# Cross-attention and mixture-of-experts block on one core: first head group's rows by tripled products, batch 1 projected later, value biases added once

## The chip, the cores and the metric

The kernel runs on one core of a Trainium2 chip. The metric is device microseconds of one execution; the value given for a kernel is the median of several runs.

## What is computed

Input x is 4 batches of 256 tokens with 128 channels, ctx is 4 batches of 64 tokens with 64 channels. All in float32; cut to what matters:

```
xn = layernorm(x)                                 # (4, 256, 128)
q, k, v = heads(xn@Wq+bq), heads(xn@Wk+bk), heads(xn@Wv+bv)        # 16 heads of 8
y  = softmax(causal(q k^T / sqrt(8))) v
qc, kc, vc = heads(xn@Wcq+bcq), heads(ctx@Wck+bck), heads(ctx@Wcv+bcv)
y += softmax(qc kc^T / sqrt(8)) vc
x1 = x + y@Wp + bp
x2 = layernorm(x1)
out = x1 + shared_expert(x2) + sum over the top 8 of 32 experts(x2)   # sigmoid router
```

## The kernel before, in words

Every product that must keep float32 precision is made of three matmuls on a rounded part ("hi") and a remainder ("lo"): hi*hi, hi*lo, lo*hi (`product3`, L1417 to L1419). So each operand is first rounded by ScalarE (`round_x`, `round_qkc`) and its remainder made by VectorE (`split_x`, `split_qkc`, which read the same PSUM bank).

**Steps.** Attention runs in 16 steps i = 4 b + g (batch b, group g of 4 heads). For one step the keys of 4 heads stand in `key_rows` (96 rows: hi, hi, lo of 32 channels) and the queries in `query_rows` (96 rows: hi, lo, hi, and 4 more rows for the shift by the row maximum). The products of a projection come out as channels x tokens in `keys` and `queries`; DMAs (`place_keys`, `place_queries`, three each for a batch and group) copy them into the rows. Context keys go by `place_ctx_keys` into `ckey_rows`. `expand(i)` multiplies the key rows by a mask per head, two heads on ScalarE and two on VectorE (POOL from step 5), and gives `key_blocks`; `expand_ctx(g)` does it for the context keys.

On TensorE, `natural(i)` makes the scores with the tokens of the queries on the partitions: tile 0 in bank B_NAT0, tile 1 in two banks, the context in B_NATC. VectorE's `maxima(i)` reduces the three (`row_max`, L1145, L1149, L1154). `turn_max(i)` (L1560) turns the maxima, ScalarE's `shift(i)` (L836) writes them into `query_rows`, `scores(i, c)` (L1574, L1579, L1583) makes the transposed scores in four parts c, and ScalarE's `exps` (L844) the probabilities. POOL's two selects clear what is above the diagonal. `attend_self`, `attend_context` (L1599 to L1611) multiply by the values, one step late. So TensorE's order in the loop is: scores(i, 0 and 1), turn_max(i+1), natural(i+2), scores(i, 2 and 3), a tail, attend(i-1). `tail_at` holds the tails: in step 0 `x_pair` (the last two batches' normalized x turned, and rounded by ScalarE), in steps 1 to 4 the projections of batches 2 and 3 (`keys_queries`, `cross_values`). The experts' part follows after step 15.

**Before step 0.** Batch 0 is projected, its rows placed by DMA (keys of group 0 by SP, queries of group 0 by ScalarE and SP, the other keys of batch 0 and all context keys from POOL's queue, the other queries from SP's). Then `natural(0)`, then all of batch 1's projections (`project(1)`), then `turn_max(0)`. The matmuls on `fill` (`run_idle`, L1457) compute nothing that is used. The norms of x are VectorE's for batches 0 and 1 (L1040) and ScalarE's for the rest (L884, after the fourth and in the midst of step 0). VectorE adds the value biases, broadcast over partitions by DMA, to every value product (L1077).

Every engine takes its instructions in the order written; waits are on semaphores.

Of the kernel before, what the change touches and what calls it, by code (L numbers as in the profile page):

```python
# [5 lines left out]
F32 = mybir.dt.float32  # L6
# [39 lines left out]
BIAS_Q, BIAS_K, BIAS_CQ, BIAS_CK = range(2 * UNITS, 2 * UNITS + 4)  # L46
BIAS_ROWS = 2 * UNITS + 4
# [23 lines left out]
B_QKC, B_VALUE, B_BIAS, B_CK = 4, 7, 2, 3  # L71
B_CV = B_OUT


FIRST_BATCHES = 2


def build(nc, x, ctx, w, out):

    with ExitStack() as stack:  # L80
# [19 lines left out]
        head_mask = sb("head_mask", [P, GROUP])  # L100
# [6 lines left out]
        w_qkv_lo = sb("w_qkv_lo", [P, 5, C], F32R)  # L107
        w_ctx = sb("w_ctx", [CTX_C, 2, C])
# [82 lines left out]
        in_wide = sem("in_wide")  # L191
# [11 lines left out]
        rows_set = sem("rows_set")  # L203
        bias_rows_set = sem("bias_rows_set")
# [3 lines left out]
        ckey_rows_set = sem("ckey_rows_set")  # L208
        zeroed = sem("zeroed")
# [27 lines left out]
        v_ckey_blocks_set = sem("v_ckey_blocks_set")  # L237
# [24 lines left out]
        have_ctxT2 = sem("have_ctxT2")  # L262
# [122 lines left out]
        def product_bank(b, n):  # L385

            if b < FIRST_BATCHES:
                return bank(B_QKC + n, SEQ)
            half = n % 2
            return psum[:, B_MISC, SEQ * half:SEQ * (half + 1)]  # L390

        def value_bank(b):

            half = b >= FIRST_BATCHES
            return psum[:, B_VALUE, SEQ * half:SEQ * (half + 1)]
# [26 lines left out]

        HALF = CHUNK // 2
# [3 lines left out]
        def rows_of_part(part):  # L427

            return slice(part, SHIFT_ROW, PARTS)

        def keys_of(b, g):

            if b == 0 and g:
                return pool_placed_k[g], 48
            return placed_k[b % 2][g], 48 * (b // 2 + (b % 2 == 1 or g == 0))

        def place_keys(eng, b, g, parts=range(PARTS)):

            mine = slice(PART * g, PART * (g + 1))
            for part in parts:  # L440
                half = KEY_PARTS[part]
                eng.dma_start(key_rows[rows_of_part(part), b % 2, g, :].bitcast(F32),
                              keys[mine, half, tokens(b)].bitcast(F32)).then_inc(keys_of(b, g)[0], 16)

        def place_queries(eng, b, g, parts=range(PARTS)):

            mine = slice(PART * g, PART * (g + 1))
            for part in parts:
                half = QUERY_PARTS[part]
                eng.dma_start(query_rows[rows_of_part(part), b % 2, g, :, :].bitcast(F32),  # L450
                              queries[mine, half, b, :, :].bitcast(F32)).then_inc(placed_q[b % 2][g], 16)

        def place_ctx_keys(eng, g):

            for part, half in enumerate(KEY_PARTS):
                eng.dma_start(ckey_rows[rows_of_part(part), g, :].bitcast(F32),  # L456
                              ckeys[PART * g:PART * (g + 1), half, :].bitcast(F32)).then_inc(placed_ck[g], 16)

        def key_block(i, j):
# [3 lines left out]
                    head_mask[0:ROWS, j:j + 1])  # L463
# [7 lines left out]
        def ckey_block(g, j):  # L471
# [3 lines left out]
                    head_mask[0:ROWS, j:j + 1])  # L475
# [34 lines left out]
        def _(sp):  # L510
# [15 lines left out]
            for n, name in enumerate(("bv", "bcv")):  # L526
                sp.dma_start(b_wide[:, n, :], row(w[name]).to_broadcast([P, C])).then_inc(in_wide, 16)
# [5 lines left out]
            sp.dma_start(bias_rows[BIAS_UP + PAIRS:BIAS_UP + UNITS, INNER:P], row(w["bu_s"])).then_inc(in_small, 16)  # L533

            sp.wait_ge(rows_set, 1)
            sp.wait_ge(qkc_rounded, 1)
            place_keys(sp, 0, 0, (0, 1))
            sp.wait_ge(qkc_split, 1)
            place_keys(sp, 0, 0, (2,))
            sp.wait_ge(qkc_split, 3)  # L540
            place_queries(sp, 0, 0, (1,))
            for g in range(1, GROUPS):
                place_queries(sp, 0, g)
# [8 lines left out]
            sp.dma_start(b_wide[:, 2, :], row(w["bp"]).to_broadcast([P, C])).then_inc(in_bp, 16)  # L552
# [14 lines left out]
        def _(pool):  # L567
# [29 lines left out]
            pool.wait_ge(x_normed, NORM_GROUPS[0][1])  # L597
            pool.memset(value[:, :, :, D:D + 1], 1.0).then_inc(zeroed, 1)
            pool.memset(ckey_rows[:, :, :].bitcast(F32), -1.0).then_inc(ckey_rows_set, 1)
            chain(pool.memset(cvalue[:, :, :, :], 0.0))  # L600
            first_rstd(1)
            pool.wait_ge(ck_rounded, 1)
            pool.wait_ge(ck_split, 1)
            pool.wait_ge(ckey_rows_set, 1)
            place_ctx_keys(pool, 0)
            pool.wait_ge(qkc_rounded, 1)
            pool.wait_ge(qkc_split, 1)
            place_keys(pool, 0, 1)
            first_rstd(2)
            place_ctx_keys(pool, 1)  # L610
            place_keys(pool, 0, 2)
            pool.wait_ge(have_rstd, 3)
            pool.memset(cvalue[0:CTX, :, :, D:D + 1], 1.0).then_inc(zeroed, 1)
            pool.wait_ge(zeroed, 2)
            pool.memset(cvalue[CTX:P, :, :, 32 + D:32 + D + 1], 1.0).then_inc(zeroed, 1)
            place_ctx_keys(pool, 2)
# [1213 lines left out]
```

## Time and profile before

| | us |
|---|---|
| median of 3 runs | 201.01 (200.78 to 201.4) |
| profiled execution, its own time | 201.61 |
| its span, from first to last instruction | 199.9 |

| engine | busy us | share of the span |
|---|---|---|
| PE (TensorE) | 187.5 | 94% |
| DVE (VectorE) | 148.6 | 74% |
| ACT (ScalarE) | 137.7 | 69% |
| POOL (GpSimd) | 111.4 | 56% |

The busy times are of the whole span. The granted TensorE clock over the span is 0.995 of full speed. 1.71 us of the profiled execution's time lie outside its span.

### The profile page before, as it was taken

What the parts mean: (1) busy time and instruction counts of PE and PEld (TensorE: products, weight loads), DVE (VectorE), ACT (ScalarE), POOL (GpSimd) and SP (SyncE); (2) the same over time, 40 slices, a digit from 0 to 9 for tenths busy, and PEclk for the clock granted to TensorE, in tenths of its full rate; (3) what the DMA queues carried; (4) which work ended last, traced back from release to release, by engine and by line L of the source; (5) the groups of instructions that cost most, each with busy time, mean ns of one, the idle gap of its engine ahead of it and who ended that gap; (6) DMA issues with size and microseconds to landing.
All of it is one profiled execution on the core that took longest, in us unless ns stands there. A gap on an engine that the chain in (4) does not pass through costs nothing.

```text
span 199.9 us, 4006 instructions
## 1 busy us (share of the span) xinstructions
PE 187.5 (94%) x1254; PEld 138.7 (69%) x1254; DVE 148.6 (74%) x343; ACT 137.7 (69%) x280; POOL 111.4 (56%) x181
## 2 busy tenths in 40 slices
PE   7969979999999999998999799699999999999993
PEld 2637657777777777765776678488788888887661
DVE  2999997677669765895692789549677888887982
ACT  3546879788898897987789375666655556555571
POOL 6889994556396699749737367685522333000020
PEclk9999999999999999999999999999999999999998
DMA  4354423222243223501111102030000000000003
GB/s 111 105 144 124 113 72 78 67 74 69 66 117 94 64 72 81 127 2 39 44 44 39 39 13 66 3 92 8 2 0 0 3 0 0 0 2 0 3 0 105
DMA packets 20434, 10.40 MB, mean 52 GB/s; under 512 B 11881, under 2 KB 18542, under 8 KB 20414
## 3 DMA queue, kind: packets, MB, share of 16 engines
q1 hardware_dynamic: 19290, 9.24, 18.4%
q0 software_dynamic: 672, 0.69, 1.4%
q10 hardware_dynamic: 452, 0.23, 0.5%
q8 instruction: 10, 0.16, 0.4%
q14 instruction: 10, 0.08, 0.1%
HBM read 4.51 MB, written 0.52 MB: 25 GB/s over the span
## 4 chain that ended last, share of the span: by engine, by line
PE 71%; DVE 12%; POOL 6%; issue 4%; ACT 4%; DMA 2%; DVEq 0%
PE psum L1417 10%; PE psum L1418 10%; PE psum L1419 10%; PE psum L1518 5%; PE psum L1574 5%; PE psum L1611 4%; PE psum L1599 4%; PE psum L1621 3%; DVE gated L1361 3%; PE psum L1517 3%; PE psum L1579 3%; PE psum L1747 3%; PE psum L1457 2%; POOL ckey_rows L456 2%; PE psum L1583 2%
## 5 line engine op out<-in xcount | busy, mean ns | idle before, releaser
L982 ACT ACTIVATE gate<-psum,bias_cols 128x512 f32<-128x512 f32 (+2 forms) x35 | 23.5, 675 | 29.1 <-PE psum L1419 29.0
L844 ACT ACTIVATE probs<-psum 128x512 f32<-128x512 f32 x64 | 36.3, 596 | 2.3 <-PE psum L1579 1.2
L1361 DVE SCALAR_TENSOR_TENSOR gated<-psum,bias_cols,gate 128x512 f32<-128x512 f32 x32 | 24.0, 749 | 13.7 <-ACT gate L982 12.9
L738 POOL TENSOR_TENSOR hid_lo<-hid,hid_hi 128x512 fp32r<-128x512 f32 x13 | 16.8, 1289 | 30.4 <-ACT hid_hi L991 30.4
L1518 PE MATMUL psum<-key_blocks,query_rows 96*128 96x512 f32 x48 | 24.1, 544 | 0.0
L1373 DVE TENSOR_TENSOR hid<-gated,psum 128x512 f32<-128x512 f32 x32 | 21.9, 683 | 2.0 <-PE psum L1747 0.2
L657 POOL TENSOR_TENSOR w_late_lo<-w_ffn,w_late_hi 128x384 fp32r<-128x384 f32 x11 | 12.7, 1158 | 17.4 <-ACT w_late_hi L856 17.4
L991 ACT CAST hid_hi<-hid 128x512 fp32r<-128x512 f32 (+1 forms) x33 | 20.2, 612 | 1.2 <-DVE hid L1379 0.6
L1145 DVE TENSOR_REDUCE row_max<-psum 128x4 fp32r<-128x512 f32 x16 | 11.0, 688 | 13.4 <-PE psum L1518 13.4
L1149 DVE TENSOR_REDUCE row_max<-psum 128x4 fp32r<-128x1024 f32 x16 | 19.4, 1214 | 0.0
L1417 PE MATMUL psum<-xT_hi,w_late_hi 128*128 128x512 f32 x42 | 16.7, 398 | 0.0
L1418 PE MATMUL psum<-xT_lo,w_late_hi 128*128 128x512 f32 x42 | 16.4, 391 | 0.0
L693 POOL TENSOR_SCALAR_AFFINE_SELECT probs<-probs 128x512 f32<-128x512 f32 x16 | 10.2, 635 | 11.2 <-ACT probs L844 11.0
L1419 PE MATMUL psum<-xT_hi,w_late_lo 128*128 128x512 f32 x42 | 16.4, 390 | 0.0
L851 ACT COPY o_sb<-psum 128x512 f32<-128x512 f32 x16 | 9.4, 585 | 9.3 <-PE psum L1611 9.2
L781 ACT ACTIVATE key_blocks<-key_rows,head_mask 100x256 fp32r<-100x256 f32 x32 | 14.4, 499 | 1.8 <-DMA key_rows<-keys 1.8
L1031 DVE TENSOR_TENSOR hid_lo<-hid,hid_hi 128x512 fp32r<-128x512 f32 (+2 forms) x22 | 14.4, 658 | 1.0 <-ACT hid_hi L991 0.9
L697 POOL TENSOR_SCALAR_AFFINE_SELECT probs<-probs 128x512 f32<-128x512 f32 x16 | 10.2, 634 | 8.5 <-ACT probs L844 8.3
L1517 PE MATMUL psum<-causal,ident_bf 128*128 128x512 bf16 x32 | 12.5, 389 | 1.8 <-DVE key_blocks L1051 1.5
L684 POOL TENSOR_TENSOR key_blocks<-key_rows,head_mask 100x256 fp32r<-100x256 f32 x22 | 13.1, 615 | 0.0
L1747 PE MATMUL psum<-routeT,spread 128*128 128x512 f32 x32 | 12.8, 401 | 0.0
L1457 PE MATMUL psum<-fill 128*128 128x512 bf16 x33 | 11.0, 458 | 1.3 <-DVE fill L1064 1.3
(208 smaller groups left out, 513.5 us busy)
## 6 DMA issues: line engine op xcount, KB each, us to landing
query_rows<-queries SPq DMA_DIRECT2D x46, 64.0 KB, 2.1
key_rows<-keys SPq DMA_DIRECT2D x39, 32.0 KB, 1.9
w_ffn<-in_L_ffn_Wg SPq DMA_DIRECT2D x16, 64.0 KB, 2.0
w_ffn<-in_L_ffn_Wu SPq DMA_DIRECT2D x16, 64.0 KB, 2.2
w_ffn<-in_L_ffn_Wd SPq DMA_DIRECT2D x16, 64.0 KB, 2.1
ckey_rows<-ckeys POOLq DMA_DIRECT2D x12, 32.0 KB, 2.1
key_rows<-keys POOLq DMA_DIRECT2D x9, 32.0 KB, 2.2
x_sb<-in_x SPq DMA_DIRECT2D x2, 128.0 KB, 2.8
```

Source lines behind the costliest of these rows:

```text
L844: act.activation(probs[:, i % 2, c, :], bank(B_ST + c % 2), ACT.Exp, scale=SCALE).then_inc(exp_done, 1)
L982: act.activation(gate[rows_of(n), n % 3, part], psum[of, B_GATE + n % 2, part], ACT.Silu, bias=bias_cols[of, BIAS_GATE + u:BIAS_GATE + u + ...
L991: act.copy(hid_hi[rows_of(n - 1), (n - 1) % 3, :], hid[rows_of(n - 1), (n - 1) % 3, :]).then_inc(hid_rounded, 1)
L1149: dve.tensor_reduce(to[:, 1, :], psum[:, B_NAT1:B_NAT1 + 2, :].rearrange("p k (j c) -> p j k c", j=GROUP), AX.XY, ALU.max).then_inc(max_do ...
L1361: dve.scalar_tensor_tensor(out=gated[:, n % 3, :], in0=bank(B_UP + n % 2), scalar=bias_cols[:, BIAS_UP + u:BIAS_UP + u + 1], in1=gate[:, n ...
L1373: dve.tensor_tensor(hid[:, n % 3, :], gated[:, n % 3, :], bank(B_WIDE + n % 2), ALU.mult).then_inc(hid_done, 1)
L1417: pe.matmul(dst, w_hi, x_hi, start=start, stop=False, skip_group_check=True)
L1418: pe.matmul(dst, w_hi, x_lo, start=False, stop=False, skip_group_check=True)
L1419: return pe.matmul(dst, w_lo, x_hi, start=False, stop=stop, skip_group_check=True)
L1517: pe.matmul(to, ident_bf[:, :], causal[:, :, :], start=True, stop=False, skip_group_check=True)
L1518: return pe.matmul(to, query_rows[0:KR, b % 2, g, 0, P * q:P * (q + 1)], blocks[:, :, P * k:P * (k + 1)], start=not diagonal, stop=True, s ...
L1747: pe.matmul(bank(B_WIDE + n % 2), spread[:, u, :], routeT[:, c * CHUNK:(c + 1) * CHUNK], start=True, stop=True).then_inc(m_wide, 1)
```

## The change

1. **Rows of step 0 without DMA.** `w_direct_hi/lo` hold the first 32 columns of Wk, Wq and Wcq three times. `project_direct(k)` multiplies them by batch 0's x, so that 96 rows come out as `key_rows` and `query_rows` of group 0 want them; `round_direct` (ScalarE) writes all 96 rows, `split_direct` (VectorE) overwrites the 32 rows that hold the remainder. Two sets of bias columns are turned, one repeated. Group 0's row order becomes part by part, so `head_mask` has two forms (`masks()`, now at VectorE's start).
2. **Queues.** SP places context keys 0 and 3, keys 1 to 3, queries 2 and 3 of batch 0; POOL places context keys 1 and 2 and queries 1. ScalarE places none.
3. **Order at the start.** Context-key product ahead of the first projection; weight remainders of Wcq and Wv on POOL; batch 1's x normalized by ScalarE, turned inside `natural(0)`; the values of batch 0 copied by ScalarE; the shift of step 0 turned and written in two halves (`first_turn`, `first_shift`).
4. **Batch 1 projected later.** `project_qkc(1, n)` stands between scores(0, 1) and natural(1); its values and the context values are a tail of step 0; `x_pair` becomes the tail of step 1; each projection of batches 2 and 3 moves one step later (steps 2 to 5). ScalarE's four norms for batches 2 and 3 move into step 1, the statistics of those batches on VectorE behind split_qkc(1, 2), their power on POOL behind the selects of step 0.
5. **Value biases.** Values are copied without a bias; `y_bias` = bv + bcv as a column is added where y is rounded and split (`y_turn`). The two broadcast loads become two rows of `bias_rows`.

The core of the diff:

```diff
-        tail_at = {0: [("x_pair", FIRST_BATCHES)]}
-        for b in range(FIRST_BATCHES, BATCH):
-            tail_at[2 * b - 3] = [("keys_queries", b)]
-            tail_at[2 * b - 2] = [("cross_values", b)]
+        tail_at = {0: [("values", 1)], 1: [("x_pair", 2)]}
+        for b in range(2, BATCH):
+            tail_at[2 * b - 2] = [("keys_queries", b)]
+            tail_at[2 * b - 1] = [("cross_values", b)]
...
@@ ScalarE, start
+            round_direct(0)
+            round_direct(1)
+            round_qkc(0, 0)
+            expand(0)
+            round_qkc(0, 1)
+            round_qkc(0, 2)
+            round_direct(2)
...
+            def first_shift(s):
+                act.wait_ge(t_max, s + 1)
+                act.copy(query_rows[SHIFT_ROW:ROWS, 0, 0, s, :],
+                         psum[0:GROUP, B_MAX, SEQ * s:SEQ * (s + 1)]).then_inc(shift_placed, 1)
...
-            shift(0)
+            act.wait_ge(have_neg_mean, 1)
+            norm(2)
+            norm(3)
+            expand_ctx(0)
+            round_x(1)
+            act.wait_ge(m_v, 1)
+            act.wait_ge(zeroed, 1)
+            act.copy(value[:, 0:2, :, 0:D],
+                     value_bank(0).rearrange("p (t h d) -> p t h d", t=2, h=HEADS)).then_inc(have_value, 1)
+            first_shift(0)
+            expand(1)
             expand_ctx(1)
-            exps(0, (0, 1))
+            exps(0, (0,))
+            first_shift(1)
+            exps(0, (1,))
             expand(2)
-            act.wait_ge(have_neg_mean, 1)
-            norm(4)
-            norm(5)
+            for n in range(3):
+                round_qkc(1, n)
             exps(0, (2, 3))
             shift(1)
-            norm(6)
-            norm(7)
             for i in range(STEPS - 2):
                 if i:
                     exps(i, (0,))
                     shift(i + 1)
                     exps(i, (1,))
+                if i == 1:
+                    act.wait_ge(have_neg_mean, 2)
+                    for t in range(4, TILES):
+                        norm(t)
                 if i + 3 < STEPS:
                     expand(i + 3)
...
@@ VectorE
+            split_direct(0)
+            split_direct(1)
+            dve.wait_ge(rows_set, 1)
+            dve.wait_ge(have_mask, 1)
+            expand(0)
+            negative_mean(1)
+            split_qkc(0, 0)
...
@@ VectorE, maxima(0)
                 tile_0()
                 if i == 0:
+                    split_qkc(0, 1)
+                    split_qkc(0, 2)
                     dve.wait_ge(m_nat, 2)
                     tile_1()
-                    values(1)
+                    split_x(1)
+                    dve.wait_ge(t_ffn_bias, 1)
+                    dve.tensor_copy(bias_cols[:, 0:LATE_BIAS_ROWS],
+                                    psum[:, B_MISC, SEQ:SEQ + LATE_BIAS_ROWS]).then_inc(have_ffn_bias, 1)
+                    split_direct(2)
+                    expand(1)
                     dve.wait_ge(m_nat, 3)
                     context()
...
             maxima(0)
+            maxima(1)
+            expand(2)
             for n in range(3):
                 split_qkc(1, n)
...
+            stats_of(2)
             for i in range(STEPS):
                 if i + 3 < POOL_BLOCKS:
                     expand(i + 3)
+                if i == 0:
+                    negative_mean(2)
                 if i + 2 < STEPS:
                     maxima(i + 2, i - 2)
...
@@ POOL, loop over the steps, after the selects
+                if i == 0:
+                    first_rstd(2)
+                    expand_ctx(3, range(GROUP))
+                    pool.wait_ge(pool_ckey_blocks_set, 12)
...
@@ TensorE, natural(0) between its tiles and its context part
+                    pe.wait_ge(qkc_split, 1)
+                    run_idle(3, B_ST)
+                    pe.wait_ge(in_small, 96)
+                    pe.transpose(psum[:, B_MISC, SEQ:SEQ + LATE_BIAS_ROWS], bias_rows[:, :],
+                                 ident[0:LATE_BIAS_ROWS, 0:LATE_BIAS_ROWS]).then_inc(t_ffn_bias, 1)
+                    turn_x(1)
+                    pe.wait_ge(qkc_split, 3)
+                    project_values(0)
+                    run_idle(3, B_ST)
+                    first_turn(0)
+                    pe.wait_ge(direct_split, 3)
...
@@ TensorE, main
             natural(0)
-            project(1)
-            turn_max(0)
-            run_idle(3, B_MISC)
+            run_idle(2, B_ST)
             for i in range(STEPS):
-                if i == 0:
-                    pe.wait_ge(qkc_split, 3 * FIRST_BATCHES)
                 scores(i, 0)
                 scores(i, 1)
                 if i == 0:
+                    pe.wait_ge(xT_split, 2)
+                    pe.wait_ge(have_ffn_bias, 1)
+                    project_qkc(1, 0)
+                    project_qkc(1, 1)
+                    pe.wait_ge(have_value, 1)
+                    project_qkc(1, 2)
                     natural(1)
-                    context_values()
-                    scores(0, 2)
                     scores(0, 3)
```

In `natural(1)` the second half of step 0's maxima is turned behind tile 0, and scores(0, 2) stands ahead of tile 1. `tail("values", 1)` is `project_values(1)` and `context_values()`.

## Rows read from the trace of the kernel before

**Rows 1.** The page: shares of the chain of waits by engine.
```profile
PE 71%; DVE 12%; POOL 6%; issue 4%; ACT 4%; DMA 2%; DVEq 0%
```

**Rows 2.** Stretches: length, busy of PE, PEld, DVE, ACT, POOL; clock; DMA share, GB/s.
```profile
7.40:14.80 7.40, 5.89 (x34) 3.61 (x34) 7.13 (x34) 3.74 (x9) 6.23 (x10) 1.00 0.46 109
14.80:19.50 4.70, 4.64 (x31) 3.26 (x31) 4.16 (x10) 2.79 (x8) 4.64 (x12) 1.00 0.52 133
19.50:28.60 9.10, 7.98 (x48) 5.45 (x48) 8.65 (x18) 7.77 (x17) 8.92 (x17) 1.00 0.38 97
28.60:140.00 111.40, 107.29 (x885) 80.64 (x886) 79.35 (x200) 87.95 (x184) 74.22 (x121) 1.00 0.24 59
```

**Rows 3.** The chain that ended last, in order of time: start, us, what.
```profile
20.95 3.65 DMA key_rows<-keys
...
26.13 0.69 DVE row_max L1145
...
28.60 0.40 PE psum L1560 x4
...
31.09 0.12 PE psum L1417
...
33.12 0.67 PE psum L1574 x4
```

**Rows 4.** Timeline of TensorE: start, us, engine, line, operation, tiles, count, idle before.
```profile
8.29 0.70 PE L1479 MATMUL psum<-ctxT,w_ctx 64*128 64x256 f32 x2
...
14.79 0.38 PE L1517 MATMUL psum<-causal,ident_bf 128*128 128x512 bf16 x1 [1.51 <-DVE key_blocks L1051]
...
19.54 0.74 PE L1574 MATMUL psum<-query_rows,key_blocks 100*128 100x256 f32 x4
...
26.38 0.60 PE L1633 MATMUL psum<-ident,x 128*128 128x128 f32 x4
```

**Rows 5.** Timeline of VectorE, 11 to 26 us.
```profile
11.36 0.86 DVE L1022 BATCH_NORM_STATS2 stats<-x_sb 128x6 f32<-128x128 f32 x4
...
12.67 0.17 DVE L1027 TENSOR_SCALAR var_eps<-moments 128x4 f32<-128x4 f32 x1
...
18.61 0.86 DVE L1086 SCALAR_TENSOR_TENSOR queries<-psum,bias_cols,queries 128x256 fp32r<-128x256 f32 x2
19.39 0.15 DVE L1288 SCALAR_TENSOR_TENSOR neg_mean<-moments,rstd 128x4 f32<-128x4 f32 x1
19.46 0.61 DVE L1051 TENSOR_SCALAR key_blocks<-key_rows,head_mask 100x256 fp32r<-100x256 f32 x2
...
24.62 1.48 DVE L1051 TENSOR_SCALAR key_blocks<-key_rows,head_mask 100x256 fp32r<-100x256 f32 x2 [0.39 <-DMA key_rows<-keys]
```

**Rows 6.** Timeline of ScalarE, 25 to 32 us.
```profile
25.27 0.88 ACT L884 ACTIVATE x<-x_sb,neg_mean,rstd 128x128 f32<-128x128 f32 x2
26.05 0.89 ACT L781 ACTIVATE key_blocks<-key_rows,head_mask 100x256 fp32r<-100x256 f32 x2
...
29.04 0.57 ACT L836 CAST query_rows<-psum 4x512 fp32r<-4x512 f32 x1 [0.94 <-PE psum L1560]
29.64 0.60 ACT L844 ACTIVATE probs<-psum 128x512 f32<-128x512 f32 x1
30.14 0.90 ACT L781 ACTIVATE key_blocks<-key_rows,head_mask 100x256 fp32r<-100x256 f32 x2
30.93 1.07 ACT L844 ACTIVATE probs<-psum 128x512 f32<-128x512 f32 x2
31.89 0.48 ACT L808 ACTIVATE keys<-psum,bias_cols 128x256 fp32r<-128x256 f32 x1
```

**Rows 7.** Timeline of POOL, 13 to 28 us.
```profile
13.82 1.21 POOL L590 TENSOR_TENSOR rstd<-var_eps,minus_half 128x4 f32<-128x4 f32 x1
...
22.97 4.74 POOL L625 TENSOR_TENSOR ckey_blocks<-ckey_rows,head_mask 100x256 fp32r<-100x256 f32 x8
```

**Rows 8.** Timeline of SP's queue, issue of three DMAs of key rows.
```profile
18.77 1.77 SPq L442 DMA_DIRECT2D key_rows<-keys  x3
```

More of the change, by code:

```diff
@@ L449, in place_queries, with place_ctx_keys @@
                 half = QUERY_PARTS[part]
[L450 to L456, printed above, removed]
+                eng.dma_start(query_rows[rows_of_part(part, g), b % 2, g, :, :].bitcast(F32),
+                              queries[mine, half, b, :, :].bitcast(F32)).then_inc(queries_of(b, g)[0], 16)
+        def place_ctx_keys(eng, g, parts=range(PARTS)):
+            for part in parts:
+                half = KEY_PARTS[part]
+                eng.dma_start(ckey_rows[rows_of_part(part, g), g, :].bitcast(F32),
                               ckeys[PART * g:PART * (g + 1), half, :].bitcast(F32)).then_inc(placed_ck[g], 16)
@@ L1018, in chain, with measure @@
                 dve.wait_ge(v_chain, chained[0])
-            def norm_stats(src, tiles, done):
+            def measure(src, tiles):
                 for k in range(tiles.start, tiles.stop):
@@ L1023, in norm_stats, with spread_of @@
                 chain(ins)
+            def spread_of(tiles, done):
                 for k in range(tiles.start, tiles.stop):
@@ L1027, in norm_stats @@
                 dve.tensor_scalar(var_eps[:, tiles], moments[:, tiles, 1], LN_EPS, None, ALU.add).then_inc(done, 1)
+            def norm_stats(src, tiles, done):
+                measure(src, tiles)
+                spread_of(tiles, done)
             def lo_half(dst, src, hi, done):
@@ L1073, in _ @@
             lo_weights(0).then_inc(w_qkv_split, 1)
[L1075 to L1081 removed]
             def split_qkc(b, n):
                 bias = ORDER[n][1]
[L1085 removed]
+                dve.wait_ge(qkc_rounded, 3 * b + max(n, b > 0) + 1)
                 dve.scalar_tensor_tensor(out=projected(b, n, 1), in0=product_bank(b, n),
@@ L1195, in tail @@
                     split_qkc(b, 1)
+                if name == "values":
+                    values(b)
+                    cvalues()
                 if name == "cross_values":
@@ L1625, in tail @@
             def tail(name, b):
-                reader = {"x_pair": xT_split, "keys_queries": qkc_split, "cross_values": have_value, "y_turn": yT_split, "project": x1_ready,
+                reader = {"values": have_value, "x_pair": xT_split, "keys_queries": qkc_split, "cross_values": have_value, "y_turn": yT_split, "project": x1_ready,
                           "x2_turn": x2T_split, "router": logits_ready,
```

432 lines of the change are left out of this document (241 added, 191 removed).

## The prediction

> **What bounds the kernel now.** I read the page's chain of waits first: TensorE has 71% of it [rows 1]. Then the chain in order of time, to see from where on nothing but TensorE stands in it: it passes through VectorE's maxima of step 2 until 28.56 us, and from `turn_max(2)` at 28.60 every piece of the attention loop that I followed, up to 60 us, is TensorE's [rows 3]. Last the stretches [rows 2]. From 28.60 to 140 us TensorE is busy 107.29 of 111.40 us; from 19.50 to 28.60 it has 7.98 of 9.10, VectorE 8.65, POOL 8.92; from 7.40 to 14.80 VectorE 7.13 of 7.40. So the kernel has a ramp, ending at `turn_max(2)`, where VectorE's and POOL's queues decide, and behind it a part where only TensorE's work and its stalls count. The change acts on the ramp and on the first steps behind it. Hence the sum: the time of `turn_max(2)` after against 28.60, plus TensorE work carried across that point, plus new stalls behind it.
>
> Durations below are start to start where two instructions follow at once, because an instruction's shown end overlaps the next start: VectorE's split of 256 columns 0.39 (18.61 to 19.39 for two), two expanded blocks 0.53 to 0.61, statistics of four tiles 1.4 to 1.48 (11.36 to 12.84) [rows 5]; three maxima 2.47 (26.13 to 28.60), so 0.6, 0.6, 1.2 [rows 3]; ScalarE's shift 0.60, one exp 0.50, two norms 0.78, two blocks 0.80, rounding 256 columns 0.36 to 0.48 [rows 6].
>
> **The ramp after.** (a) *First scores.* In the rows before, the context-key product starts at 8.29 behind two projections of 6 x 0.12 us [rows 3, 4], so these began at about 7.5. Now it (0.70) and a second bias turn (0.2, estimated) precede them: the first direct projection starts at about 8.35. ScalarE rounds it at 8.75, done 9.2; VectorE splits it to 9.7, splits the next to 10.1, expands two blocks to 10.6; ScalarE, behind `round_direct(1)` and `round_qkc(0, 0)`, expands its two to 10.7. `natural(0)`: 10.8 instead of 14.79 [rows 4], 4.0 earlier. The DMA of group 0's rows, and VectorE's statistics, copies and context blocks that stood ahead, no longer lie on this way.
>
> (b) *To scores(0, 0).* VectorE: 0.65 for the first tile's products, tile 0 0.6, two splits 0.8, tile 1 1.13, `split_x(1)` 0.33, bias copy 0.1, `split_direct(2)` 0.39: 14.85. TensorE waits for that (direct_split 3) ahead of the context scores (0.25), then two idle matmuls 0.45: scores(0, 0) at 15.6, against 19.54 [rows 4]: 3.9 earlier. ScalarE in that time has nine instructions (three roundings, two norms, two context blocks, the turned x, the values: some 3.6 us) and is ready for `first_shift(0)` at 14.65.
>
> (c) *Step 1.* What followed `natural(0)` before (batch 1's projections) now follows scores(0, 1): 0.67 for scores, 9 x 0.12 = 1.07 for products, then `natural(1)` with its half turn, context part and scores(0, 2), 1.9. Its last product lands at 19.45. ScalarE: `exps(0, 0)` at 16.65 (behind two expands), then `first_shift(1)` at 18.15, so exps(0, 1) waits behind that shift until 18.5; it ends at 19.0, before TensorE wants it at 19.3. VectorE ends tile 1 of step 1 at 20.6.
>
> (d) *To turn_max(2): here the lead goes.* VectorE still has, in order: expand(2) 0.53, three splits of batch 1 1.17 (before they filled its waits ahead of step 0), statistics of the last four tiles 1.39: 23.7. Its `negative_mean(2)` then waits for POOL's power, 1.21 for four columns [rows 7], issued only when these statistics are there: 25.0, behind it 0.15. `expand(3)` (0.53) fits into that wait. Then the maxima of step 2, 2.47: `turn_max(2)` at 27.6. I add 0.2, since two blocks took 1.48 and not 0.61 while POOL multiplied its own blocks beside them [rows 5, 7]: **27.8, 0.8 us earlier than before**. Bounds: with every duration taken as shown instead of start to start, and two such slow pairs, 28.8; with the power wholly hidden 26.4. TensorE, waiting, does the context values and batch 1's values (1.6) in this hole.
>
> *Queues.* SP issues 21 DMAs for batch 0 instead of 10, at 0.59 each [rows 8], from 8.6 on. Keys 1 are down by 14.2, keys 3 by 21.3 (wanted 23.7), and its first key rows of batch 1 are issued by 24.3, down at 26.3 and wanted by VectorE's expand(4) at about 29.3. So I cost it at nothing; if it were 3 us late, step 4 would wait. POOL issues 9 instead of 21. Before, one transfer of its queue ended 3.65 us after its issue and VectorE's expand(3) waited for it [rows 3, 5]; that wait goes. The Trainium skill ("SBUF — State Buffer", the part on DVE blocking SWDGE transfers) says that a transfer issued from GpSimd needs descriptors which GpSimd cannot write while VectorE holds the shared port. By that rule the nine left on POOL may each take as long as that one; queries 1, issued at 13.0, would land at 16.7, and they are wanted at 17.35. So by the rule nothing is lost as long as the queue runs as I laid it out, and from 0.7 us of lag on `natural(1)` would slip with it; it speaks for a few hundredths of B's chance below.
>
> **Behind turn_max(2).** (e) `x_pair`, done before 28.60 in the old order [rows 4], is now behind it: four transposes, the row's 0.60 less the overlap with what follows, **+0.45**. The projections of batches 2 and 3 are the same work one step later: nothing. (f) ScalarE's four norms were spread over step 0, where it had time (7.77 busy of 9.10 [rows 2]). Now they stand in step 1 behind shift(2) and exps(1, 1), and `x_pair` needs them. From `turn_max(2)`: shift starts at +0.44, exp at +1.04, norms at +1.54, four of them 1.56 and an end: +3.2. TensorE reaches the tail of step 1 at 31.09 - 28.60 = +2.49 [rows 3]. **Stall +0.8**. Behind the norms ScalarE has expand(4) 0.80, exps(1, 2) and (1, 3), the turned x 0.5, a copy 0.5, then exps(2, 0) and shift(3), which then ends about when `natural(4)` asks for it (+7.0 against +6.8): 0 taken, 0.5 as upper bound. With full durations in place of starts the stall is 1.1.
>
> (g) *Value biases.* Two broadcast loads fall away that nothing waited for; values are copied in place of added, same size; `y_turn` gets a column bias in ScalarE's rounding (no cost) and a three-operand split in VectorE (0.43 where a plain one has 0.33 to 0.42), four times, with VectorE at 79.35 of 111.40 [rows 2]: nothing. If that cover were gone, 0.4 in all.
>
> **Sum.** -0.8 + 0.45 + 0.8 = +0.45. On the profiled execution's own 201.61 (span 199.9 and 1.71 outside) that is 202.05; the median of the runs is 201.01, 0.6 below it, so the forecast is 201.01 + 0.45, **201.5**. Its own range: 200.9 to 202.3. Below 0.3% (0.6 us) a difference can't be told from none.
>
> **Rivals.**
> *A, faster: VectorE's queue does not hold `turn_max(2)`.* If what VectorE does in (d) fits into waits, TensorE's own order sets it: 15.6 + 0.7 + 1.07 + 1.9 + scores(0, 3), a turn and `natural(2)` 2.4, values 1.6, scores(1) 0.7, gives 24.4, that is -4.2 + 0.45 + 0.8, or 198.1. For it: the lead of 3.9 at scores(0, 0) is large, and the slowed pair and the late DMA vanish. Against: VectorE was busy 8.65 of 9.10 before, and the work it did ahead of step 0 is only moved. It decides from `turn_max(2)` at 26.7 downward; half the lead kept gives 199.6. Chance 0.26.
> *B, slower: ScalarE becomes the bound in steps 1 and 2.* Ramp at its upper bound (28.8) because the longer ScalarE row (first_shift(1) ahead of exps(0, 1), roundings ahead of exps(0, 2)) delays POOL's selects and VectorE's splits, and stall (f) at 1.1 + 0.5: +2.2, or 203.2. For: ScalarE works 4 to 5 of every 5.2 us step, so a lag of 1 us is caught up slowly. Against: a step's order still leaves it 0.4 to 0.8 of slack. It decides once `turn_max(2)` is later than 28.2. Chance 0.26.
> *C, no change by the norms:* TensorE's tail finds them ready, or loses under 0.2 us; -0.8 + 0.45: 200.7. Chance 0.12.
> The forecast has 0.36.
>
> Clock: in every stretch of [rows 2] the granted clock is the higher level, 2.4 GHz. The new order leaves one idle matmul fewer ahead of the first projections; at 1.2 GHz the two direct products would cost 0.7 more, and the ramp with them, at most +0.7. It is inside B's price.
>
> **How the numbers follow.** Faster by over 0.3%: nearly all of A and a little of C: 0.29. Within: C and more than half of the forecast's case: 0.31. Slower: the rest of it and B: 0.40. Range 199.0 to 203.1: half of A's lead kept is inside, and so is nearly all of B.
>
> **What would show it.** (a) `natural(0)`'s first product at 10.3 to 11.3; (b) scores(0, 0) at 15.1 to 16.3; (d) VectorE's maxima of step 2 begin when POOL's power is done, near 25.2, and `turn_max(2)` stands at 27.3 to 28.8; (f) the four norms lie between exps(1, 1) and expand(4), and TensorE is idle 0.5 to 1.1 ahead of the transposes of `x_pair`; from there on the steps take as long as before. Wrong if `turn_max(2)` comes before 26.7 (then faster), if DMAs of SP are what VectorE or ScalarE wait for, or if a later step has a wait for ScalarE that the trace before does not have.

## Result: slower, and by more than forecast

| | before | after |
|---|---|---|
| median of 4 runs, us | 201.06 (200.78 to 201.4) | 207.42 (205.47 to 207.76) |
| ratio, 95% interval | | 1.0292 (1.0261 to 1.0323) |
| profiled execution, its own time | 201.61 | 207.49 |
| its span | 199.9 | 205.6 |
| mean granted TensorE clock | 0.995 | 0.965 |

The forecast was 201.5 with a range of 199.0 to 203.1; the time is outside it. Where executions of one kernel differ much (e2, e7, e8, e12 below), the ratio is that of the less disturbed ones, so it isn't the quotient of the medians.

### The profile page after: what moved, and what is told of

Its sections match the earlier page's. It is cut to its first block, busy times and chain, and to the rows that moved or that the text cites. A ratio compares the mean times of both kernels' runs of the same rounds, so it can differ in the third digit from the quotient of the medians.

```text
span 205.6 us, 4019 instructions
## 1 busy us (share of the span) xinstructions
PE 192.7 (94%) x1244; PEld 143.4 (70%) x1256; DVE 151.0 (73%) x338; ACT 141.2 (69%) x292; POOL 108.9 (53%) x175
## 4 chain that ended last, share of the span: by engine, by line
PE 68%; DVE 12%; POOL 10%; issue 5%; ACT 4%; DVEq 0%; POOLq 0%
PE psum L1524 10%; PE psum L1525 9%; PE psum L1526 9%; PE psum L1629 6%; PE psum L1706 4%; PE psum L1731 4%; PE psum L1743 4%; PE psum L1753 3%; PE psum L1711 3%; DVE gated L1468 3%; PE psum L1882 3%; POOL ckey_blocks L669 2%; PE psum L1715 2%; PE psum L1628 2%; DVE hid L1480 2%
## 5 line engine op out<-in xcount | busy, mean ns | idle before, releaser
L1629 PE MATMUL psum<-key_blocks,query_rows 96*128 96x512 f32 x48 | 25.7, 578 | 0.0
L744 POOL TENSOR_SCALAR_AFFINE_SELECT probs<-probs 128x512 f32<-128x512 f32 x16 | 10.2, 638 | 14.7 <-ACT probs L921 14.7
L1706 PEld LDWEIGHTS psum<-query_rows,key_blocks 100*128 100x128 f32 x64 | 9.1, 197 | 5.2 <-issue 4.9
L1706 PE MATMUL psum<-query_rows,key_blocks 100*128 100x256 f32 x64 | 12.5, 318 | 0.0
```

The costliest lines, as they stand in the source:

```text
L1629: return pe.matmul(to, query_rows[0:KR, b % 2, g, 0, P * q:P * (q + 1)], blocks[:, :, P * k:P * (k + 1)], start=not diagonal, stop=True, s ...
L1706: ins = pe.matmul(psum[:, to, SEQ * j:SEQ * (j + 1)], key_blocks[0:ROWS, i % RING, 2 * c + j, 0:P], query_rows[0:ROWS, b % 2, g, 0, :], st ...
```

## The profile after

The page, busy tenths and granted clock in 40 slices of the span:

```profile
PE   7989699999999999998999899899999999999993
PEclk9999855899999999999999999999999999999999
```

TensorE looks well used throughout, but in four slices of 5.14 us each, from 20.6 to 41 us, the granted clock is at 8, 5, 5 and 8 tenths of full speed. So a full digit of PE there is slow work. The same stretch cut finer, columns as in [rows 2]:

```profile
16.00:20.30 4.30, 4.30 (x32) 3.43 (x30) 3.50 (x6) 3.43 (x9) 4.09 (x9) 1.00 0.36 88
20.30:21.10 0.80, 0.18 (x1) 0.00 (x0) 0.80 (x2) 0.80 (x3) 0.80 (x3) 1.00 0.09 22
21.10:21.60 0.50, 0.40 (x4) 0.21 (x4) 0.50 (x2) 0.50 (x2) 0.50 (x2) 1.00 0.18 49
21.60:22.90 1.30, 0.00 (x0) 0.00 (x0) 1.30 (x3) 1.25 (x4) 1.10 (x2) 1.00 0.41 101
22.90:23.90 1.00, 0.94 (x5) 0.71 (x5) 1.00 (x3) 0.86 (x2) 0.00 (x0) 0.93 0.27 66
23.90:28.10 4.20, 4.20 (x17) 3.66 (x16) 3.46 (x15) 0.00 (x0) 2.59 (x4) 0.50 0.28 70
...
29.70:36.50 6.80, 6.80 (x38) 4.71 (x37) 4.45 (x9) 5.05 (x11) 2.34 (x4) 0.50 0.33 81
...
37.00:37.60 0.60, 0.60 (x4) 0.00 (x0) 0.00 (x0) 0.00 (x0) 0.00 (x0) 0.66 0.21 55
```

TensorE works without a pause until 20.3, then 0.58 of the next 2.6 us. It resumes at 22.9 at the full clock and falls to half of it, 1.2 GHz, before 23.9. It comes back after 37.0, although from 29.7 on it was never idle. In the kernel before, the clock is 1.00 in every stretch of [rows 2].

Why TensorE had nothing to do: VectorE's timeline of the same stretch (start, us, what),

```profile
19.83 1.23 DVE L1253 TENSOR_REDUCE row_max<-psum 128x4 fp32r<-128x1024 f32 x1 [0.28 <-PE psum L1629]
20.98 1.88 DVE L1172 TENSOR_SCALAR key_blocks<-key_rows,head_mask 100x256 fp32r<-100x256 f32 x2
22.78 0.47 DVE L1200 SCALAR_TENSOR_TENSOR keys<-psum,bias_cols,keys 128x256 fp32r<-128x256 f32 x1
...
25.34 0.61 DVE L1172 TENSOR_SCALAR key_blocks<-key_rows,head_mask 100x256 fp32r<-100x256 f32 x2
26.62 0.58 DVE L1142 SCALAR_TENSOR_TENSOR neg_mean<-moments,rstd 128x4 f32<-128x4 f32 x1 [0.67 <-POOL rstd L638]
27.12 0.68 DVE L1249 TENSOR_REDUCE row_max<-psum 128x4 fp32r<-128x512 f32 x1
```

and POOL's:

```profile
19.14 2.33 POOL L669 TENSOR_TENSOR ckey_blocks<-ckey_rows,head_mask 100x256 fp32r<-100x256 f32 x4
21.42 0.69 POOL L744 TENSOR_SCALAR_AFFINE_SELECT probs<-probs 128x512 f32<-128x512 f32 x1
...
25.51 1.07 POOL L638 TENSOR_TENSOR rstd<-var_eps,minus_half 128x4 f32<-128x4 f32 x1 [2.81 <-DVE var_eps L1124]
26.57 2.31 POOL L669 TENSOR_TENSOR ckey_blocks<-ckey_rows,head_mask 100x256 fp32r<-100x256 f32 x4
```

Two expanded blocks take 0.61 at 25.34, where POOL stands still and then runs its power of 128x4 elements (25.51), and 1.88 at 20.98, beside POOL's context blocks and selects; `neg_mean` takes 0.58 instead of 0.15 [rows 5] beside the next context blocks. `natural(2)` needs the two blocks of 20.98 and starts when they are done. TensorE's timeline at that point, and the chain around `turn_max(2)` (L1690) and `turn_max(3)`:

```profile
21.11 0.40 PE L1690 MATMUL psum<-ident_r,row_max 128*4 128x128 f32 x4 [0.63 <-DVE row_max L1253]
22.96 0.38 PE L1628 MATMUL psum<-causal,ident_bf 128*128 128x512 bf16 x1 [1.44 <-issue]
```

```profile
28.32 1.22 DVE row_max L1253
29.54 0.08 issue
29.62 0.63 PE psum L1561
30.25 0.43 PE psum L1690 x4
...
34.58 0.85 PE psum L1768 x4
...
38.36 0.24 PE psum L1690 x4
```

`turn_max(2)` is at 30.25 where before it was at 28.60 [rows 3]. VectorE is done at 29.54; the idle matmuls ahead of it (L1561) are short work that at half the clock ends only at 30.25. The way from `turn_max(2)` to `turn_max(3)` is 8.11 us, where it was 5.19 before (28.60 to 33.79); 0.85 of the 8.11 is `x_pair` (L1768), which before wasn't in it. At `turn_max(7)` the two kernels are 5.29 apart (60.83 against 55.54), at the end of the span 5.7.

## Experiments

In every kernel an edit is shown against the kernel after, unless it says otherwise. "Fill" is matmuls on `fill` whose product nobody reads.

### e1_fill: is it the clock?

```diff
@@ TensorE, natural(i), ahead of step 2
                     pe.wait_ge(max_done, 3 * i)
+                    if i == 2:
+                        run_idle(6, B_NAT0)
@@ turn_max(i)
-                    run_idle(2, B_NAT0)
+                    run_idle((2, 5, 7)[i], B_NAT0)
@@ loop over the steps
             for i in range(STEPS):
+                if i == 1:
+                    pe.wait_ge(exp_done, 3)
+                    run_idle(4, B_ST)
                 scores(i, 0)
```

> The changed kernel with more idle matmuls and nothing else: six ahead of natural(2), five instead of two and seven instead of two in the first turns of the maxima, four ahead of the scores of step 1. Theory T (the loss is TensorE's clock, which fell to the lower level 1 us after the hole of 1.3 us ahead of natural(2) and stayed there until 37.3 us): the clock holds at 1.00 to 40 us, turn_max(2) stays near 29.6, since VectorE sets it, and the rest is 1.0 (ramp) + 0.45 (x_pair) + 0.8 (norms) above the kernel before: 203.3 us. Rival R (the loss is the order behind turn_max(2), above all the waits for ScalarE, and the clock only reflects it): stays within 1 us of 207.4 us.

Measured: 204.74 us (204.35 to 205.1); ratio 1.0169 (1.0149 to 1.019). Windows of this kernel:

```profile
20.00:24.00 4.00, 3.85 (x21) 2.01 (x21) 4.00 (x9) 3.35 (x8) 2.34 (x4) 1.00 0.25 60
24.00:29.00 5.00, 4.76 (x30) 3.07 (x28) 4.26 (x14) 0.60 (x1) 3.79 (x6) 1.00 0.29 72
29.00:38.00 9.00, 8.14 (x68) 6.10 (x69) 6.96 (x15) 8.17 (x18) 3.30 (x8) 1.00 0.31 78
```

With work that computes nothing the clock stays at 1.00 and 2.7 us of the median come back. `turn_max(7)` is at 57.62, 3.21 before that of the kernel after. Not all of that is the clock: VectorE's last maxima of step 1, long before the clock falls, are already 0.37 earlier in this execution than in the one of the kernel after (19.83),

```profile
19.46 1.22 DVE L1253 TENSOR_REDUCE row_max<-psum 128x4 fp32r<-128x1024 f32 x1 [0.27 <-PE psum L1631]
```

and so are its last maxima of step 2 (27.95 against 28.32). So the clock's price in the profiles is 2.84, close to the 2.7 of the medians, and 0.37 is how early an execution comes to this point. What is left above before, 2.08 at `turn_max(7)`, is a ramp of +0.61 (`turn_max(2)` 29.21) and 1.47 behind it, in which a wait shows that the slow clock had covered (first ScalarE's norms, then TensorE's transposes of `x_pair`):

```profile
30.74 1.64 ACT L963 ACTIVATE x<-x_sb,neg_mean,rstd 128x128 f32<-128x128 f32 x4
```

```profile
31.25 0.45 PE L1717 MATMUL psum<-query_rows,ckey_blocks 100*128 100x256 f32 x2
32.52 0.63 PE L1770 MATMUL psum<-ident,x 128*128 128x128 f32 x4 [0.82 <-ACT x L963]
```

TensorE's pause comes to 0.98 if the two context products ahead of it are counted at the 0.29 that they take in the chain (the bracket, which counts shown ends, has 0.82). The median is 1.4 above what was expected. Against before, the profiled executions differ by 2.08 at `turn_max(7)`, by 2.5 in the span and by 2.74 in their own times, the medians by 3.64 (201.10 for before, measured beside e1). Of the last step 0.51 is that the profiled execution of before lies above this median, 0.39 that e1's lies below its own.

### e2_pool: POOL beside expand(2)

```diff
@@ POOL, start
+            expand_ctx(2, range(GROUP))
             pool.memset(cvalue[:, :, :, :], 0.0).then_inc(zeroed, 1)
...
-            pool.wait_ge(zeroed, 4)
-            expand_ctx(2, range(GROUP))
```

> The changed kernel with POOL's four context blocks of group 2 ahead of its clears of cvalue, so that they don't run beside VectorE's expand(2). Theory T2 (expand(2) took 1.88 us and not 0.61 because POOL multiplied its blocks at the same time; that delay made the hole): expand(2) takes 0.6 to 0.8 us, natural(2) starts by 21.8, the maxima of step 2 come 1.2 us earlier, and if the clock holds the kernel takes 202 us; with the clock fallen all the same 206. Rival (VectorE's slow instruction has another cause): 1.9 us again and 207.4 us.

Measured: 205.56 us; its four executions 206.54, 203.16, 205.16, 205.95 at mean clocks of 0.975, 0.997, 0.982, 0.974; ratio 1.0171 (1.0105 to 1.0237). The two blocks of expand(2), and a window ahead of `turn_max(2)` and one behind it, of the execution with 206.54:

```profile
21.04 0.61 DVE L1172 TENSOR_SCALAR key_blocks<-key_rows,head_mask 100x256 fp32r<-100x256 f32 x2
```

```profile
26.00:28.00 2.00, 0.53 (x1) 0.11 (x2) 2.00 (x3) 0.36 (x1) 1.94 (x4) 0.74 0.29 68
28.00:36.00 8.00, 7.62 (x41) 4.84 (x41) 5.23 (x10) 5.05 (x11) 2.83 (x7) 0.50 0.32 80
```

The context blocks were what stretched expand(2): 1.88 to 0.61, with `turn_max(2)` at 28.38 and the maxima of step 2 beginning 1.2 earlier, as expected. But the clock now falls in the second hole, while TensorE waits for these maxima. One execution escaped (mean clock 0.997) and took 203.16.

### e3_fill_norms: the stall of x_pair

e1 with the norms moved to the end of step 0:

```diff
-                if i == 1:
-                    act.wait_ge(have_neg_mean, 2)
-                    for t in range(4, TILES):
-                        norm(t)
                 if i + 3 < STEPS:
                     expand(i + 3)
+                if i == 0:
+                    act.wait_ge(have_neg_mean, 2)
+                    for t in range(4, TILES):
+                        norm(t)
```

> As e1_fill, and ScalarE's four norms of batches 2 and 3 stand at the end of step 0 behind expand(3), in its wait for the scores of step 1. If the norms in step 1 cost a stall ahead of x_pair, as predicted, this is 0.5 to 0.9 us below e1_fill; if the stall was hidden, the same as e1_fill.

Measured: 203.89 us (203.39 to 204.11), 0.85 less than e1; ratio 1.0124 (1.01 to 1.0148). The transposes of `x_pair` follow without a wait (no bracket in the row):

```profile
32.00 0.60 PE L1770 MATMUL psum<-ident,x 128*128 128x128 f32 x4
```

So the stall is real and costs about what it shows, as expected. `turn_max(2)` to `turn_max(7)` is 27.24 us here, 28.41 in e1, 26.94 before: 0.3 of it is `x_pair`. In this execution expand(1) took 2.93 beside POOL (1.79 in e1), which put `turn_max(2)` at 29.83.

### e4_before_noidle: holes of another size

The kernel before, without nine idle matmuls:

```diff
@@ TensorE, turn_max(i)
-                if i < 2:
-                    run_idle(2, B_MISC)
-                if i == 2:
-                    pe.wait_ge(have_cvalue, 2)
-                    run_idle(2, B_OUT)
...
-            run_idle(3, B_MISC)
             for i in range(STEPS):
```

> The kernel before without the nine idle matmuls that stand in the first three turns of the maxima and behind the first one, nothing else. Theory T: they hold the clock in the ramp; without them a hole of 2 to 3 us opens ahead of turn_max(2), the clock falls to the lower level for some 10 us, and the time is 3 to 5 us above the kernel before. Rival: the ramp is set by VectorE and POOL, the idle matmuls do nothing for the time, within 0.5 us of 201.0.

Measured: 201.27 us (200.94 to 201.88, 10 runs); ratio 1.0008 (0.9995 to 1.0021).

```profile
24.00:26.00 2.00, 1.17 (x6) 0.62 (x5) 1.41 (x4) 1.95 (x5) 1.66 (x3) 1.00 0.20 55
26.00:28.40 2.40, 1.65 (x16) 1.32 (x14) 2.40 (x4) 1.87 (x4) 2.33 (x5) 1.00 0.40 99
```

The expectation was wrong: TensorE is busy 2.82 of 4.40 us here, and the clock holds (over the ten executions its mean is 0.986 to 1.0). The order before isn't saved by its idle matmuls; it has no hole as deep as 0.58 of 2.60. Why it holds here is not shown, though: in e11 below it fell behind 1.13 of 2.00, close to the 1.17 of 2.00 here. The trace also serves as a second look at the order before. Its chain has `turn_max(2)` at 28.05 and `turn_max(7)` at

```profile
54.99 0.24 PE psum L1555 x4
```

both 0.55 before those of the profiled execution of before, with the same 26.94 between them.

### e5_no_value_bias: part 5 by itself

The kernel before, with the values copied and no bias added to them:

```diff
-            for n, name in enumerate(("bv", "bcv")):
-                sp.dma_start(b_wide[:, n, :], row(w[name]).to_broadcast([P, C])).then_inc(in_wide, 16)
...
-                dve.tensor_tensor(dst, src, which, ALU.add).then_inc(done, 1)
+                dve.tensor_copy(dst, src).then_inc(done, 1)
```

> The kernel before with the value biases left out altogether: no broadcast loads of bv and bcv, values and context values copied where a bias was added. It gives the upper bound of what part 5 of the change can bring. My step (g) said nothing: within 0.4 us of the kernel before. Rival (the loads crowd the start of the ramp, or the additions lengthen VectorE's queue ahead of the maxima): 0.5 us or more below it.

Measured: 201.16 us (10 runs); ratio 0.9998 (0.9987 to 1.001). Leaving the value biases away altogether (the result is then another) gains nothing, as expected; so nothing was to be had from part 5.

### e6_stats_pool and e7_three_moves: repair the queues

e6 is e2 and in addition:

```diff
@@ VectorE
             maxima(0)
+            stats_of(2)
             maxima(1)
...
-            stats_of(2)
@@ POOL, start, behind expand_ctx(2)
+            first_rstd(2)
@@ POOL, step 0
-                    first_rstd(2)
```

e7 is e6 with the norms in step 0, as in e3.

> The changed kernel with POOL's context blocks of group 2 ahead of its clears, and VectorE's statistics of the last four tiles ahead of the maxima of step 1, in the hole that VectorE has there, with POOL's power behind the blocks of group 2. Theory S (in the ramp it was the chain statistics, power, neg_mean behind the splits of batch 1, and expand(2) beside POOL's blocks, that held turn_max(2)): the maxima of step 2 start at 23.5 to 24 instead of 27.1, turn_max(2) stands at 26 to 26.5, and the kernel takes 199.5 to 200.5 us with the norms' stall of 0.8 to 1.0 still in it. Rival (VectorE is simply full, or ScalarE's roundings behind exps(0, 1) come last): turn_max(2) not before 27.5, 201.5 us or more.

> As e6, and ScalarE's four norms at the end of step 0 behind expand(3). Expected 0.5 to 1.0 us below e6 (the stall ahead of x_pair goes), 198.7 to 199.6 us and below the kernel before, if the clock holds without more idle matmuls. If the clock falls as in the changed kernel: 202 or more.

Measured: e6 202.44 us (202.25 to 203.01), ratio 1.007 (1.0053 to 1.0088). e7 201.63 us, ratio 1.0019 (1.0008 to 1.003); eight of its ten executions took 201.13 to 201.87, two 205.38 and 205.6 at a mean clock of 0.975. Both expectations failed: e6 was to take 199.5 to 200.5 and e7 198.7 to 199.6, and `turn_max(2)`, expected at 26 to 26.5, is at 27.12 in e6 and at 27.69 in e7. Only the step from e6 to e7, 0.81, came as expected. VectorE's two pairs of blocks in e7, and POOL's row beside the first:

```profile
21.22 1.43 DVE L1172 TENSOR_SCALAR key_blocks<-key_rows,head_mask 100x256 fp32r<-100x256 f32 x2
...
23.75 1.06 DVE L1172 TENSOR_SCALAR key_blocks<-key_rows,head_mask 100x256 fp32r<-100x256 f32 x2
```

```profile
21.06 1.18 POOL L679 MEMSET cvalue<- 128x1312 f32 x1
```

The clear that took the place of the context blocks slows the two blocks as well, 1.43 (the same in e6). With the statistics ahead, the way from the end of the splits to `neg_mean` is 0.99 in e6, where it was 2.67 in e2; 0.82 of that was lost again in expand(2), beside the clear.

### e8, e9, e10: fill again, and a late clear

e8 and e9 are e7 with fill, e9 at all three places of e1:

```diff
@@ e8, turn_max(i)
-                    run_idle(2, B_NAT0)
+                    run_idle((2, 4, 2)[i], B_NAT0)
@@ e9, natural(2), turn_max(i), ahead of scores(1, 0)
+                        run_idle(5, B_NAT0)
...
-                    run_idle(2, B_NAT0)
+                    run_idle((2, 4, 5)[i], B_NAT0)
...
+                    run_idle(2, B_ST)
```

e10 is e9 without the fill ahead of `natural(2)`, and with the clears late:

```diff
@@ POOL, start
-            pool.memset(cvalue[:, :, :, :], 0.0).then_inc(zeroed, 1)
...
-            pool.memset(cvalue[CTX:P, :, :, 32 + D:32 + D + 1], 1.0).then_inc(zeroed, 1)
@@ POOL, step 0
                     pool.wait_ge(pool_ckey_blocks_set, 12)
+                    pool.memset(cvalue[:, :, :, :], 0.0).then_inc(zeroed, 1)
...
+                    pool.memset(cvalue[CTX:P, :, :, 32 + D:32 + D + 1], 1.0).then_inc(zeroed, 1)
```

> As e7 with two more idle matmuls in turn_max(1), which fill the hole ahead of the maxima's turn. If e7's clock holds: the same as e7 within 0.3 us. If it doesn't: 2 to 4 us below e7.

> As e7 (statistics early, POOL's blocks of group 2 ahead of its clears, norms in step 0), with idle matmuls in the three holes that its trace still shows: five ahead of natural(2), two more and three more in the turns of step 1 and 2, two ahead of scores(1). Two of e7's ten executions took 205.4 to 205.6 us at a mean clock of 0.975, the others 201.1 to 201.9 at 0.996 to 1.0. Theory (those were executions in which the clock fell in the holes): no execution over 202.5 us, the median at 201.4. Rival (another state of the chip): still one or two in ten at 205.

> As e9, and POOL's clears of cvalue behind the blocks of group 3, so that they don't run beside expand(2), which took 1.43 us in e7 and 0.61 in e2. If VectorE's queue still sets the ramp: turn_max(2) at 26.9 instead of 27.7, 0.6 to 0.9 us below e9 and below the kernel before (200.6). If shift(1) or ScalarE's norms come last: within 0.3 us of e9.

| | median, us | ratio | executions of 205.2 to 205.6 |
|---|---|---|---|
| e7 | 201.63 | 1.0019 (1.0008 to 1.003) | 2 of 10 |
| e8 | 201.59 | 1.0017 (1.0005 to 1.0029) | 3 of 10 |
| e9 | 201.72 | 1.0027 (1.0012 to 1.0042) | 0 of 11 |
| e10 | 201.04 | 0.9999 (0.9984 to 1.0013) | 0 of 11 |

Two idle matmuls more in one turn don't help. Of the three long executions of e8 two have a mean clock of 0.982 and 0.981, but the third, 205.2, has 0.997: the fall of the clock doesn't explain that one, and nothing kept does. With fill in all the holes no execution of e9 is long, as expected, nor is one of e10. e10 takes 0.7 off e9, as expected, and is the best version, but it doesn't reach the expected 200.6: it is as fast as the kernel before, not faster. The 0.7 isn't the late clear's alone. VectorE ends the maxima of step 2 only 0.22 earlier (27.15 against 27.37); in both kernels `turn_max(2)` then still waits behind idle matmuls, 0.44 in e9 and 0.21 in e10. In e10's chain everything from `turn_max(1)` to `turn_max(2)` is TensorE's, 1.64 of it idle matmuls; fewer of them weren't tried. Its expand(2) still isn't alone; a select of POOL (20.85 to 21.48) runs beside it:

```profile
21.00 0.90 DVE L1172 TENSOR_SCALAR key_blocks<-key_rows,head_mask 100x256 fp32r<-100x256 f32 x2
```

`turn_max(2)` is at 27.36, 1.24 before that of before; at `turn_max(7)` 0.94 of it is left (`x_pair` took 0.3), in the span 0.5, in the medians nothing. Against e4's trace of the order before, the lead at `turn_max(7)` is 0.39 and the span the same, 199.4.

### e11 and e12: one hole filled at a time

```diff
@@ e11, natural(2)
+                        run_idle(6, B_NAT0)
@@ e12, turn_max(i), and ahead of scores(1, 0)
-                    run_idle(2, B_NAT0)
+                    run_idle((2, 2, 7)[i], B_NAT0)
...
+                    run_idle(4, B_ST)
```

> The changed kernel with six idle matmuls ahead of natural(2), in the hole of 1.44 us in which nothing ran on TensorE, and nothing else. If that hole is what lowers the clock: 204.5 to 205 us as e1. If the holes behind it matter as well (ahead of turn_max(2)): in part of the executions or in all 206 to 207.5 us.

> The changed kernel with idle matmuls ahead of scores(1) and in turn_max(2) alone (four, and seven instead of two). The clock has fallen by then if the first hole does it, and these matmuls run at the lower level: 207 to 208 us. If the second hole is the one that counts: 204.5 to 205 us.

Measured: e11 206.53 us (206.03 to 207.82), ratio 1.0272 (1.0232 to 1.0313). e12 207.09 us, executions 207.01, 207.17, 204.55, 208.37 at clocks 0.982, 0.982, 1.0, 0.982. Windows of e11:

```profile
22.00:26.00 4.00, 3.90 (x24) 2.73 (x23) 3.93 (x15) 2.00 (x5) 1.20 (x3) 1.00 0.26 63
26.00:28.00 2.00, 1.13 (x9) 0.80 (x7) 1.33 (x3) 0.60 (x1) 2.00 (x4) 1.00 0.36 89
28.00:30.00 2.00, 1.17 (x4) 0.27 (x5) 2.00 (x4) 0.00 (x0) 1.84 (x6) 0.51 0.28 72
```

and of e12:

```profile
20.00:22.50 2.50, 0.77 (x6) 0.21 (x4) 2.50 (x3) 2.48 (x7) 2.50 (x5) 1.00 0.18 43
22.50:24.00 1.50, 1.14 (x7) 0.84 (x7) 1.50 (x5) 1.14 (x3) 0.10 (x1) 0.88 0.37 90
24.00:30.00 6.00, 5.67 (x22) 4.56 (x23) 5.26 (x17) 0.00 (x0) 4.04 (x8) 0.50 0.26 66
30.00:32.00 2.00, 2.00 (x12) 1.20 (x11) 1.13 (x4) 0.60 (x1) 0.00 (x0) 0.89 0.42 100
```

With the first hole filled the clock stays until 28 and falls in the second, before TensorE has resumed; in e12 it falls after the first as in the kernel after. So each hole can be enough by itself. Of the kernel after, e1, e3, e11 and e12, only e1 and e3, with both holes filled, kept the clock up in every execution; in e12 it stayed up in one of four. In e12 it also comes back sooner, at 30.5. TensorE's fill there:

```profile
28.46 1.49 PE L1561 MATMUL psum<-fill 128*128 128x512 bf16 x3 [0.34 <-issue]
...
30.55 1.69 PE L1561 MATMUL psum<-fill 128*128 128x512 bf16 x7
```

The seven in `turn_max(2)` began only when it was back, and they and the four ahead of `scores(1, 0)` (three are in the trace) stood in the way of late work: `turn_max(2)` is at 32.23, 3.02 behind e1. So e12's time is the slow clock and idle matmuls together.

## Why the prediction was wrong

**(a), (b), (c) held.** `natural(0)` at 11.03 (forecast 10.8), scores(0, 0) at 15.88 (15.6), VectorE's maxima of step 1 done at 21.06 (20.6). So the change does what it says: 3.7 us of lead at the first scores. In (a) two errors met, which is luck: the first direct projection started at 7.73 and not at 8.35, and the way from it to `natural(0)` took 3.3 us and not 2.45.

**(d), "I add 0.2", was too small by far.** From the end of those maxima VectorE's expand(2) took 1.80 until the next start instead of 0.53; splits and statistics took 1.17 and 1.39 as forecast, POOL's power 1.07 instead of 1.21, `neg_mean` 0.50 instead of 0.15. The maxima of step 2 began at 27.12 instead of 25.15: 0.46 from the later start, 1.27 from expand(2), 0.35 from `neg_mean`, the rest small. The term should have been 1.6, not 0.2, and the upper bound of 28.8 for `turn_max(2)` was passed too, even with the clock held (29.21 in e1). The trace before had the row for it, 1.48 for two blocks [rows 5] beside POOL's [rows 7]; I had read it as an exception instead of asking what POOL would run at 21 us. e2 shows that POOL's context blocks do it, e7 that a clear does it too. The Trainium skill ("SBUF — State Buffer", "Who interferes with whom") says that VectorE, in a two-port mode or with two operands in SBUF (then only against a GpSimd instruction that reads SBUF), and GpSimd exclude each other on a shared port for whole instructions, and that the one issued second waits. Which mode the blocks run in no row shows. The rows agree in kind, 0.61 against 1.43 beside the clear and 1.88 beside the context blocks; I had weighed only that page's other rule, on transfers from POOL's queue, which no row after shows: the transfers of query rows, three of them POOL's, landed in 1.9 to 2.3 us.

**The sentence on the clock is the step that failed.** "It is inside B's price" looked only at the start, where one idle matmul fewer stands ahead of the projections; there nothing happened. The forecast itself had the hole in it ("TensorE, waiting, does the context values and batch 1's values (1.6) in this hole") and didn't ask what the clock does behind it. Between the kernel after and e1, `turn_max(7)` differs by 3.21 us: 1.04 at `turn_max(2)` (30.25 against 29.21) and 2.17 more up to `turn_max(3)`. Less the 0.37 by which e1's execution was ahead before the clock fell, the fall costs 2.84. By medians it is 2.7. Price and bound of the clock in the forecast, "at most +0.7", were for the start alone. None of the rivals had it, so the range ended at 203.1. Without it the ramp alone is +0.61 in e1's execution, and +0.98 in that of the kernel after if the 0.37 is put to it, instead of -0.8.

**(e)** `x_pair`, +0.45: 0.3 (e3, e10) to 0.5 (e1, without its stall). **(f)** Stall +0.8: 0.98 in e1, and 0.85 off the median without it (e3). In the kernel after it can't be seen, since TensorE at half the clock arrives later than the norms. ScalarE costs nothing in the later steps: `turn_max(3)` to `turn_max(7)` is 22.47 us after, in e1 and in e3 alike, so rival B had the direction and not the mechanism. Two slips stand in the rivals: the terms of A add up to 24.0 and not 24.4, and B's own 203.2 lies just outside the range that was said to hold nearly all of B. **Queues:** nothing waited for SP's transfers. **(g)** e5 shows that the removed additions gave nothing. Where y is rounded and split there is a small cost that I had put at none. The last pair before, and after:

```profile
118.55 0.36 ACT L791 CAST yT_hi<-psum 128x256 fp32r<-128x256 f32 x1
119.25 0.41 DVE L1031 TENSOR_TENSOR yT_lo<-psum,yT_hi 128x256 fp32r<-128x256 f32 x1
```

```profile
123.98 0.47 ACT L948 ACTIVATE yT_hi<-psum,y_bias 128x256 fp32r<-128x256 f32 x1
124.66 0.47 DVE L1316 SCALAR_TENSOR_TENSOR yT_lo<-psum,y_bias,yT_hi 128x256 fp32r<-128x256 f32 x1
```

They are 0.11 and 0.06 longer, and the chain that ended last passes through the split, so up to 0.1 or 0.2 of the end may be theirs; no experiment shows it.

**The sum after the fact,** at `turn_max(7)` in profiled executions: ramp +0.98, `x_pair` and stall +1.47, clock +2.84, together 5.29. Up to the end of the span the new order loses some 0.4 more, in the kernel after (5.7), in e1 (2.5 against 2.08) and in e10 (0.94 to 0.5) alike; apart from the split of y I have no cause for it.

**Open:** e1's median lies 3.64 above before's where its terms give 2.08. Most of that is which executions were profiled: against e4's, which stands nearer to its median, the terms give 2.63 at `turn_max(7)`, with 0.4 behind it, and 0.39 is that e1's lies below its own median. The time outside the span also differs, 1.75 to 2.07 in the kernels of the new order, 1.68 to 1.82 in the old. What makes the executions differ in the ramp is not shown (expand(1) took 1.79 in e1's profile and 2.93 in e3's). Nor is it shown what decides in which executions the clock falls.

## What to carry to other kernels

A lead at the first step is worth nothing if the queue that ends the ramp isn't shortened: here 3.7 us of lead became holes on TensorE. Price such a hole twice, once as time and once as clock, and fill it or move work into it before judging the change; here one filled hole wasn't enough, since another followed. Before moving VectorE's work on SBUF, look at what POOL runs at that moment, and lay the two queues out together.

## What the runs showed of the hardware

- In the kernel after the granted clock fell from 2.4 to 1.2 GHz 0.8 us after TensorE had resumed, behind 2.6 us in which it was busy for 0.58, and stayed there for 13.6 us (23.8 to 37.4), although from 29.7 on TensorE worked without a pause, in float32 and narrow matmuls. In e2 it fell at 27.0, 0.1 us after TensorE had resumed, in e11 at 28.1, while TensorE was still idle, and stayed there for 10.2 us in both; in e12 for 6.8 us (23.6 to 30.5).
- Whether it falls differs between executions of one kernel: 203.16 at a mean clock of 0.997 and 206.54 at 0.975 for e2, 204.55 at 1.0 and 207.01 at 0.982 for e12, 201.13 at 1.0 and 205.6 at 0.975 for e7. The Trainium skill ("TensorE: Matmul & The Clock Gate", "What's actually happening") says that how many matmuls run at the lower level at the start of a kernel differs from run to run; here executions of one kernel differ in the midst of it.
- Two VectorE blocks of 100 x 256 took 0.61 us alone or beside POOL's power of 128 x 4, 0.90 beside a select, 1.43 beside a clear, and 0.96 (e3) to 2.93 beside POOL's multiplications, which covered them in part or in whole. `neg_mean`, 128 x 4, took 0.15 us, and 0.57 to 0.58 beside these.
